# Head attention of a four-stage block: side jobs of TensorE moved between key tiles, one small VectorE product in another form

## The reference, cut to what matters

```python
x = x + _L0_xattn_ref(_layernorm(x), ctx, mask, mask, Wq, bq, Wk, bk, Wv, bv)

q = einsum('oc,bct->bot', Wq, target) + bq      # target: normalised x, 256 channels x 512 positions
k = einsum('oc,bcs->bos', Wk, source) + bk      # source: ctx
v = einsum('oc,bcs->bos', Wv, source) + bv
dot = einsum('bhdt,bhds->bhts', q, k) / sqrt(16)                 # 16 heads of 16 channels
dot = mask * dot - (1 - mask) * 1e6
amap = softmax(dot, axis=-1) * mask
out = einsum('bhts,bhds->bhdt', amap, v)
```

## Time and profile before

| what | before |
|---|---|
| median of three runs | 1445.33 us |
| the profiled execution, its own time | 1449.05 us |
| its span | 1447.2 us |
| loop over the 8 sequences, in the trace | 200 to 682 us |
| TensorE busy over the span | 91% |
| VectorE, ScalarE, GpSimd busy over the span | 70%, 45%, 21% |

### The profile page before, as it was taken

The page is one execution under the profiler, slowest core; times in us unless marked ns, Lnnn a source line. Parts: engine busy times, 40 slices in busy tenths (PEclk is TensorE's granted clock), DMA queues, the critical chain, the costliest instruction groups (busy, mean ns, idle before and its releaser), DMA issues.

```text
span 1447.2 us, 23348 instructions
## 1 busy us (share of the span) xinstructions
PE 1314.5 (91%) x9142; PEld 753.9 (52%) x9142; DVE 1019.0 (70%) x1523; ACT 649.7 (45%) x941; POOL 297.0 (21%) x473
## 2 busy tenths in 40 slices
PE   5788868898988989886999989999999999999998
PEld 2344412222222222222767767787777777777776
DVE  8999778889898897884777856644467544575353
ACT  5776537777787877783453111232111321112210
POOL 1018255545455554220000000000000000000000
PEclk9999969999999999996999999999999999999999
DMA  6300222333334323232744301000010000100000
GB/s 201 106 18 23 73 70 91 109 88 101 106 93 147 99 81 101 62 122 67 267 129 143 104 30 59 13 18 1 30 60 2 30 1 15 63 12 30 1 1 30
DMA packets 78038, 101.23 MB, mean 70 GB/s; under 512 B 14679, under 2 KB 51647, under 8 KB 77927
## 3 DMA queue, kind: packets, MB, share of 16 engines
q1 hardware_dynamic: 75879, 99.43, 21.8%
q0 software_dynamic: 2048, 0.27, 0.1%
HBM read 78.07 MB, written 21.34 MB: 69 GB/s over the span
## 4 chain that ended last, share of the span: by engine, by line
PE 39%; DVE 9%; DMA 2%; ACT 1%; issue 1%; POOL 1%; POOLq 0%; DVEq 0%; ACTq 0%; SPq 0%
PE double L1800 13%; PE double L1814 11%; PE double L1826 5%; PE double L1879 3%; PE double L1847 3%; PE double L1836 2%; PE double L1866 1%; DVE stats L1987 1%; PE double L1784 1%; DVE f1w L2092 1%; DVE hid L2034 1%; DMA x_early<-scr_x 1%; DVE gate L2032 1%; DMA out_x<-x_early 1%; DVE x_early L2003 1%
## 5 line engine op out<-in xcount | busy, mean ns | idle before, releaser
L1029 ACT ACTIVATE prob<-level,head_scale 128x512 f32<-128x512 f32 x512 | 319.2, 683 | 92.4 <-PE level L946 92.2
L1390 DVE TENSOR_REDUCE nmx<-level 128x2 f32<-128x1024 f32 x256 | 304.9, 1221 | 56.3 <-PE level L936 56.0
L1912 ACT ACTIVATE th<-double 128x512 f32<-128x512 f32 x96 | 54.0, 563 | 384.7 <-PE double L1800 211.6
L946 PE MATMUL level<-stacks 59*128 59x512 f16 x512 | 175.0, 390 | 24.5 <-ACT prob L1029 24.2
L936 PE MATMUL level<-stacks 57*128 57x512 f16 x512 | 150.7, 394 | 11.6 <-DVE nmx L1390 10.9
L374 PE MATMUL level<-prob,x_parts 128*128 128x512 bf16 x540 | 126.4, 389 | 34.9 <-DVE prob L421 18.0
L1800 PE MATMUL double<-x_parts,f0w 128*128 128x256 f16 x1408 | 156.3, 274 | 1.6 <-PEq L521 1.6
L1973 POOL TENSOR_TENSOR rstd<-meanvar,halfpow 128x2 f32<-128x2 f32 x22 | 15.2, 691 | 689.7 <-DVE meanvar L1993 689.7
L1800 PE MATMUL double<-x_parts,f1w 128*128 128x256 f16 x1408 | 155.2, 273 | 0.9 <-DVE hid L2034 0.9
L1800 PEld LDWEIGHTS double<-x_parts,f0w 128*128 128x128 bf16 x1408 | 138.2, 98 | 20.3 <-issue 2.1
L1800 PEld LDWEIGHTS double<-x_parts,f1w 128*128 128x128 bf16 x1408 | 137.6, 98 | 18.9 <-DVE hid L2034 1.2
(11 more groups left out here) (254 smaller groups left out, 1878.3 us busy)
## 6 DMA issues: line engine op xcount, KB each, us to landing
stacks<-scr_q SPq DMA_DIRECT2D x64, 96.0 KB
stacks<-scr_k SPq DMA_DIRECT2D x64, 96.0 KB
hid<-in_f1w1t SPq DMA_DIRECT2D x8, 704.0 KB, 6.7
hid<-in_f1w2t SPq DMA_DIRECT2D x8, 704.0 KB, 4.2
inputs<-in_x SPq DMA_DIRECT2D x8, 512.0 KB, 7.3
inputs<-in_ctx SPq DMA_DIRECT2D x8, 512.0 KB, 7.0
scr_q<-splits SPq DMA_DIRECT2D x16, 256.0 KB, 2.4
scr_k<-splits SPq DMA_DIRECT2D x16, 256.0 KB, 2.1
```

The lines of the kernel that those rows point to most:

```text
L946: nc.tensor.matmul(pB[n % 2], Ks[rows, g, j // 2, P * c:P * (c + 1)], Qs[rows, g, j // 2, :], start=True, stop=True).then_inc(s["b_pe"], 1)
L1029: nc.scalar.activation(prob[:, c, j, :], pB[(64 * b + 16 * g + 4 * c + j) % 2], ACT.Exp, scale=hscale[:, 10:11]).then_inc(s["exp_done"], 1)
L1390: nc.vector.tensor_reduce(nmx[:, g % 2, :, half, tt], pA[(32 * b + 8 * g + u // 2) % 2], AX.X, ALU.max, negate=True).then_inc(s["max_done" ...
L1912: y = nc.scalar.activation(th[:, 0:m, :], src[:, 0:m, 0:S], ACT.Tanh, scale=0.5 / XS)
```

## The change: the job table, where its readers stand, and one product

`MISC` gets its jobs one to a tile, in the first half, with the two o jobs as the only pair: k of channels 0 goes from (0,0) to (0,3), the o jobs from (0,3) to (1,0), q and k of channels 1 from (1,0) to (1,3) and (2,0), and the second v job from (2,3) to (3,0). The readers on ScalarE, VectorE and GpSimd follow (`PROJECTED` is new), the loop of SyncE's queue issues the fill of group 1 before the stores of the second half, and line 1419 is written as a `scalar_tensor_tensor` with a multiplication by 1.0 in place of a `tensor_tensor`.

```diff
--- before.py
+++ after.py
@@ -634,12 +634,14 @@
 
 
         MISC = {
-            (0, 0): [("q", 0, 1), ("k", 0, 1)], (0, 1): [("nm", 1, 0), None], (0, 2): [("t", 3, -1), None],
-            (0, 3): [("o", 0, -1), ("o", 1, -1)],
-            (1, 0): [("q", 1, 1), ("k", 1, 1)], (1, 1): [("nm", 2, 0), None], (1, 2): [("t", 0, 0), None],
-            (2, 1): [("nm", 3, 0), None], (2, 2): [("t", 1, 0), None], (2, 3): [("v", 0, 1), ("v", 1, 1)],
-            (3, 1): [("nm", 0, 1), None], (3, 2): [("t", 2, 0), None],
+            (0, 0): [("q", 0, 1), None], (0, 1): [("nm", 1, 0), None], (0, 2): [("t", 3, -1), None], (0, 3): [("k", 0, 1), None],
+            (1, 0): [("o", 0, -1), ("o", 1, -1)], (1, 1): [("nm", 2, 0), None], (1, 2): [("t", 0, 0), None],
+            (1, 3): [("q", 1, 1), None],
+            (2, 0): [("k", 1, 1), None], (2, 1): [("nm", 3, 0), None], (2, 2): [("t", 1, 0), None], (2, 3): [("v", 0, 1), None],
+            (3, 0): [("v", 1, 1), None], (3, 1): [("nm", 0, 1), None], (3, 2): [("t", 2, 0), None],
         }
+
+        PROJECTED = {(0, 0): (0, 0), (0, 3): (0, 1), (1, 3): (1, 0), (2, 0): (1, 1)}
 
         LAST = {(2, 1): [None, ("rep", 0, 0)], (2, 3): [None, ("one", 0, 0)], (3, 0): [("x", 0, 0), None],
                 (3, 1): [("top", 0, 0), None], (3, 3): [("spread", 0, 0), None]}
@@ -817,9 +819,8 @@
                     sp.wait_ge(s["out_done"], 2 * b + 1)
                     sp.dma_start(x1_t[b - 1], xres[:]).then_inc(s["out_store"], 16)
                 if not last:
+                    fill(b + 1, 1)
                     store_parts(b + 1, 1)
-                    fill(b + 1, 1)
-                if not last:
                     fill(b + 1, 2)
 
                 sp.wait_ge(s["out_store"], 16 * (b + 1))
@@ -1055,8 +1056,9 @@
                 for g in range(NG):
                     for c in range(DK):
                         exps(b, g, c, 0)
-                        if c == 0 and g < 2 and not last:
-                            q_evac(b + 1, g, (0,))
+                        if (g, c) in PROJECTED and not last:
+                            i, n = PROJECTED[g, c]
+                            q_evac(b + 1, i, (n,))
                         if c == 1:
                             if g:
                                 av_evac(b, g - 1)
@@ -1067,8 +1069,6 @@
                             elif not last:
                                 nm_evac(b + 1, 0)
                         exps(b, g, c, 1)
-                        if c == 0 and g < 2 and not last:
-                            q_evac(b + 1, g, (1,))
                         if last and (g, c) == (3, 0):
                             act.wait_ge(s["x_turned"], 1)
                             nc.scalar.activation(xh.rearrange("p k t -> p (k t)"), turned2.rearrange("p a b -> p (a b)"),
@@ -1201,8 +1201,10 @@
             def body(b, first, last, ending):
 
                 for g in range(NG):
-                    if not last and g < 2:
-                        split(b + 1, g, (0,))
+                    if not last and g == 0:
+                        split(b + 1, 0, (0,))
+                    if not last and g == 2:
+                        split(b + 1, 1, (1,))
                     if g < NG - 1:
                         max_rows(b, g + 1)
                     elif not last:
@@ -1212,7 +1214,7 @@
                     elif not last:
                         value_group(b + 1, 0)
                     if not last and g < 2:
-                        split(b + 1, g, (1,))
+                        split(b + 1, g, (1 - g,))
                     if g == 1 and not ending:
                         ln_pow(b + 2)
                     if g == 2 and not ending:
@@ -1416,8 +1418,8 @@
                 t4 = pM[:].rearrange("p (t j c) -> p t j c", t=DK, c=32)
                 nc.vector.reciprocal(rs[:], t4[:, :, :, HD]).then_inc(s["t_a"], 1)
                 dve.wait_ge(s["t_a"], 2 * e + 1)
-                nc.vector.tensor_tensor(rs[:], rs[:], mcol[:, :, b].unsqueeze(2).broadcast_to([P, DK, G]),
-                                        ALU.mult).then_inc(s["t_a"], 1)
+                nc.vector.scalar_tensor_tensor(rs[:], rs[:], 1.0, mcol[:, :, b].unsqueeze(2).broadcast_to([P, DK, G]),
+                                               ALU.mult, ALU.mult).then_inc(s["t_a"], 1)
                 dve.wait_ge(s["t_a"], 2 * e + 2)
                 if g == 0:
                     wait(dve, s["o_pe"], 2 * b)
@@ -1474,7 +1476,7 @@
                                     normalise(b, g - 1)
                                 elif not first:
                                     normalise(b - 1, NG - 1)
-                            if g == 0 and c == 3 and not first:
+                            if g == 1 and c == 0 and not first:
                                 residual(b - 1, (half,))
                             if last and half:
                                 if (g, c) == (2, 0):
@@ -1498,8 +1500,8 @@
                                     dense_norm(1)
                                 elif (g, c) == (3, 3):
                                     attention_scales()
-                            if g == 2 and c == 3 and not last:
-                                v_evac(b + 1, half)
+                            if (g, c) in ((2, 3), (3, 0)) and half == 0 and not last:
+                                v_evac(b + 1, g - 2)
                         if g == 0 and c == 3 and not ending:
                             ln_stats(b + 2)
                         if g == 1 and c == 3 and not ending:
```

## The result

The changed kernel takes **1460.83 us** in the median of six runs (1457.82 to 1462.52), the kernel before 1445.12 in its six. The ratio is 1.0106, with a 95% interval of 1.0096 to 1.0117: **1.1% slower**, where 1.3% faster was forecast, outside the range of 1410 to 1436. The profiled execution took 1462.24 us, its span is 13.2 us longer than before. One of the ten executions of a later experiment, the statistics later alone, took 4440.94 us, and its time there is the median of the other nine.

A forecast was written before the change was run, and what follows sets the result against it. Each tile was taken as a chain of score, exponential, score and value product, with neither TensorE nor ScalarE full. Terms of -2.36 us per sequence in 1 to 5, plus sequences 0 and 6, gave -19.1: 1426.2 us, range 1410 to 1436.

The forecast's parts named there:

- A job in a first half costs 0.42 us: Any tile: a job in TensorE's first-half hole costs 0.42 us, behind the value product 1.40, so each move wins 0.98.
- (0,1) to (1,0), -2.38: These four tiles of a sequence take 14.18 us in place of 16.56, with (1,0) at 4.36.
- The wait of (1,1), at nothing: Tile (1,1): the nm job waits for the second residual, covered by ScalarE's two copies; cost 0, uncovered some 0.4 us.
- (2,1), the added wait: Tile (2,1): VectorE's ln_apply waits 3.3 us for GpSimd's power behind the split of q; +2.55 us per sequence.
- The rival of a longer stall: GpSimd's split of k also holds up ln_apply: six stalls grow by 1.28 us, 7.7 in all, 1433.9 us; chance 0.15.
- The DMAs, at nothing: Later store of k and the group fills: cost 0, though first row scores of (2,1) might wait if cover is gone.
- The product's form: Product of inverse sums and mask as scalar form: term 0, up to -1.2 us if it didn't wait for GpSimd.
- The rival that ended slower: First-half jobs cost in full, 1.40 us in place of 0.42, adding 41.2 us: 1467.4 us; chance 0.10.

The follow-up runs named there:

- the statistics later alone: Changed kernel with only VectorE's layer norm statistics moved from behind tile (0,3) to behind (1,0), the power staying late: 1446.25 us, ratio 1.0016.
- The last experiment: Kernel before with only the second v job moved, from the second half of (2,3) to the first half of (3,0): 1437.62 us, ratio 0.9952.
- the filled kernel: Changed kernel plus eight unread TensorE products in tile (2,1) of sequences 0 to 5, during the wait for VectorE: 1448.45 us, ratio 1.0029.

## Why the prediction was wrong

Point by point, by its own steps.

- *A job in a first half costs 0.42 us*: right. (0,0) and (3,0) came to 0.01, (0,3) and (1,3) to 0.07. The last experiment shows the count alone. (2,0) is 0.27 more (3.75), and its lines show why: in tile (1,3) ScalarE reads q and is still behind with the exponentials, so the second column score of (2,0) waits, and the k job starts 0.81 us in and not 0.54. (3,0) follows a job tile too, but VectorE reads the v jobs, and it takes 3.49.

```profile
355.63 0.37 PE L947 MATMUL level<-stacks 59*128 59x512 f16 x1
...
356.44 1.47 PE L879 MATMUL pM<-context_parts,wk_parts 128*128 128x512 f16 x6
...
354.13 0.78 ACT L1013 ACTIVATE splits<-pM,bq,head_scale 128x512 f32<-128x512 f32 x1 [0.36 <-PE pM L879]
354.81 2.50 ACT L1030 ACTIVATE prob<-level,head_scale 128x512 f32<-128x512 f32 x4
...
356.11 0.09 PEld L947 LDWEIGHTS level<-stacks 59*128 59x128 f16 x1 [0.39 <-ACT prob L1030]
```

- *(0,1) to (1,0), -2.38*: the sum left out 0.77 us in (1,0), 5.13 for 4.36. The statistics end with an operation that GpSimd's split of k holds up for 0.81 us, since k is now projected in the very tile behind which they stand. The prediction reckoned them at 1.67 us, a length from a trace in which no split ran beside them. The two o jobs and the residuals are as counted; without the layer norm, in sequence 6, (1,0) takes 3.63 for a forecast of 3.65.
- *The wait of (1,1), at nothing*: the nm job waits 0.96 us, which costs 0.15 at full clock (3.42 and 3.43 for 3.28), so its cover held. But in sequences 2, 3 and 5 the clock falls to half during this wait, and (1,1) takes 4.84 to 4.92.
- *(2,1), the added wait*: the place and the mechanism were right, 3.2 us of VectorE behind the power that stands behind the split of q. The size was not: +2.55 forecast, 4.0 to 5.0 measured. Without the hold and at full clock it is 5.38 - 3.28 = 2.1. That is 0.45 less than the sum has, but 0.34 of it is only that (1,3) and (2,0) came out longer: (2,2) starts 12.7 us behind the start of (1,3), forecast 12.79. So the waits were sized rightly. The hold of the norm's application adds 1.40 (6.78 against 5.38) where both are held, about 0.95 where only the first is, and the clock the rest.
- *The rival of a longer stall* held just that mechanism, priced at 1.28 us a stall, at a chance of 0.15 and against the reason that the application reads one tensor of SBUF. That reason is wrong: line 1336, with one tensor as its input, takes 1.49 us beside the split and 0.54 without it.
- **The step that failed for the sign** is one that the sum didn't have: a stall of TensorE was priced at its length, in the +2.55 of (2,1), or at nothing, in (1,1). In this kernel the granted clock fell to half behind most of them. Of the 5.7 us that sequences 1 to 5 took on average over their forecast (62.08 less 56.39), 2.1 are holds and small terms, since the two sequences of the filled kernel at full clock take 58.47, and, by estimate, **3.6 are the clock and what its delay brings**. The estimate isn't clean. The filled kernel's longer hold of the application makes it some 0.3 too small. The wait for the input in sequence 4 makes it some 0.1 too large. And about 0.4 of it is GpSimd's longer hold of the delayed product in (2,2): the v job waits for what follows it, and (2,3) takes 3.61 to 4.56 us in place of 3.49. At 58.47 each of those five sequences would have been 0.3 us faster than before, beside the 5 of sequence 6, so by this estimate the clock turned the sign; no run has the changed kernel's waits at full clock throughout. Filling the stall won 12.4 us and didn't free all sequences of half clock, and that kernel is still 0.3% slower than the one before. Of the 34.6 us between forecast and result, sequences 1 to 5 hold about 28.4, sequence 0 6.1 and sequence 6 0.4, by the profiled executions.
- *The DMAs, at nothing*: right for the fills, none of which is waited for. But the load of the layer norm's input, which the prediction doesn't speak of, is late in sequence 4 by 1.37 us.
- *The product's form*: right, at nothing. In groups 0 and 1 the long ones went with the split; the one in (2,2) stayed, 1.49 to 1.88 us.
  The Trainium skill, SBUF — State Buffer, section Who interferes with whom, has a case for both holds. One is a VectorE instruction with two inputs in SBUF against a GpSimd instruction that reads SBUF, with no exception for a form; this case agrees, 1180 ns against 1191 in the median. The other is a tensor_scalar in a mode that uses both of VectorE's port pairs. No run shows the mode of lines 1336 and 1239, but they are held, 1.49 and 0.98 us beside a split step, 0.54 and 0.17 without.
- *The rival that ended slower* was not what happened; its price (jobs in full) is refuted by the tiles. That its 1467.4 lies near the measured 1460.8 is chance.

What stays open: why the same waits were followed by a fall of the clock in some sequences and not in others. (1,0) took 5.13 us in sequences 1 and 2 of the changed kernel, with the clock whole in (1,1) of the first and at half in the second (3.42 and 4.84 us). Nor is it known why the second application is held in some sequences and not in others: in both kinds GpSimd's cast starts 0.09 to 0.10 us behind it.

## What to carry to other kernels

Moving a job moves everything that stands in order behind its readers: list, on every engine, what is queued behind the moved reader, and put first what another engine waits for; here one small power ahead of a split was worth 34 us. Stalls of TensorE of 1 to 3 us cost more than their length here: look at the granted clock behind them, and at the length of the same matmul before and after. And whenever two engines' small operations come to lie side by side, ask whether one holds the other up, since lengths from a trace in which they didn't meet don't show it.

## What the runs showed of the hardware that was not expected

- In sequence 2 TensorE's clock went from 2.4 to 1.2 GHz at 345.5 us, behind a wait of 1.43 us and within one of 0.96, and at 362.5, 0.2 us behind the end of a wait of 2.54. It doesn't follow each such wait: in sequence 3 the clock stayed whole for 2 us behind a wait of 2.54. Eight useless products in a wait, 1.90 us of work, made the kernel 12.4 us faster.
- VectorE's tensor_scalar on 128x2 elements took 0.98 us beside a GpSimd operation, 0.17 alone; on 128x512, 1.49 against 0.54. In sequence 2 the short one ended at 341.81 us, GpSimd's operation beside it at 341.79; the application from 359.08 ended within 0.3 us of the split's step that ends at 360.28.
- GpSimd can be lengthened in VectorE's place: in sequences 2, 3 and 5 of the changed kernel the split's cast took 0.92 us (at 360.58 in sequence 2) and the second application beside it 0.54; in 0, 1 and 4 the cast took 0.62 and the application 0.99.
